# Edge steps of the mixing stage: three doubled instead of six, eight index places, a new order of the last loads, and the low half of the gathered sources on VectorE

## The reference

```python
xn = _layernorm(x, axis=-1)
x = x + gnn(xn) + mix(xn)      # below
x = x + ffn(_layernorm(x))     # eight experts, the best one per node, weighted by its gate

def _sage_conv(x, src, dst, W_l, W_r, b):
    n = x.shape[0]
    summed = jax.ops.segment_sum(x[src], dst, num_segments=n)
    deg = jax.ops.segment_sum(jnp.ones((src.shape[0],), x.dtype), dst, num_segments=n)
    agg = summed / jnp.maximum(deg, 1.0)[:, None]
    return agg @ W_l.T + x @ W_r.T + b

h = jnp.tanh(_sage_conv(xn, src, dst, W1_l, W1_r, b1))
gnn = _sage_conv(h, src, dst, W2_l, W2_r, b2)

z = 1.0 / jnp.einsum('bnhf,bhf->bnh', q_phi, k_phi.sum(axis=1))
mix = jnp.einsum('bnhf,bhfd,bnh->bnhd', q_phi, kv, z) @ w_proj + b_proj
```

## Time and profile before

| | before |
|---|---|
| median of 3 runs | 2524.41 us |
| profiled execution, its time | 2524.75 us |
| its span, first to last instruction | 2522.9 us |
| TensorE busy | 2373.8 us (94%) |
| VectorE busy | 1693.2 us (67%) |
| GpSimd busy | 1185.5 us (47%) |
| mixing stage, its products | about 1515 to 2121 us |

### The profile page before, as it was taken

The page is one execution under the profiler, slowest core; times in us unless marked ns, Lnnn a source line. Parts: engine busy times, 40 slices in busy tenths (PEclk is TensorE's granted clock), DMA queues, the critical chain, the costliest instruction groups (busy, mean ns, idle before and its releaser), DMA issues.

```text
span 2522.9 us, 37535 instructions
## 1 busy us (share of the span) xinstructions
PE 2373.8 (94%) x11499; PEld 1899.0 (75%) x11499; DVE 1693.2 (67%) x3522; ACT 1110.6 (44%) x2047; POOL 1185.5 (47%) x1087
## 2 busy tenths in 40 slices
PE   5899999999999999899999988989999997886997
PEld 4788888888888888688888865666777776664986
DVE  5577777777777774444443337778888784994676
ACT  3345554444444443343443433333332331664875
POOL 5576776666666664000000004555565551775444
PEclk8999999999999999999999998999999998998999
DMA  9865765555555554455445436887888777995885
GB/s 370 265 186 156 201 162 143 147 145 126 143 145 129 142 146 103 194 210 201 178 157 199 184 131 195 210 221 215 237 230 235 218 216 267 353 367 212 253 262 190
DMA packets 159280, 507.40 MB, mean 201 GB/s; under 512 B 30274, under 2 KB 30786, under 8 KB 127026
## 3 DMA queue, kind: packets, MB, share of 16 engines
q1 hardware_dynamic: 109380, 376.45, 41.7%
q0 software_dynamic: 49200, 128.35, 23.2%
q10 hardware_dynamic: 576, 1.07, 0.1%
HBM read 263.83 MB, written 241.96 MB: 200 GB/s over the span
## 4 chain that ended last, share of the span: by engine, by line
PE 82%; DMA 7%; DVE 3%; issue 3%; SPq 2%; ACT 2%; POOL 1%; ACTq 0%; POOLq 0%; DVEq 0%
PE bank L1352 54%; PE bank L1403 8%; PE bank L1359 6%; DMA agg_d<-O,eidx 4%; PE bank L1536 3%; PE bank L1612 3%; PE bank L1467 2%; PE bank L439 1%; PE bank L440 1%; ACT r_xn L962 1%; SPq L509 1%; PE bank L1602 1%; DVE pd L1182 1%; PE bank L1604 1%; DMA a_x<-in_x 1%
## 5 line engine op out<-in xcount | busy, mean ns | idle before, releaser
L400 POOL DMA_INDIRECT agg_d<-O,eidx x160 | 274.2, 1714 | 210.2 <-DMA agg_d<-O,eidx 144.6
L336 POOL TENSOR_TENSOR G_low<-G,G_high 128x512 fp32r<-128x512 f32 x160 | 235.2, 1470 | 237.8 <-ACT G_high L461 237.6
L383 POOL DMA_INDIRECT G<-y_d,esrc x80 | 87.4, 1093 | 527.6 <-DMA y_d<-b_y 514.9
L419 DVE SCALAR_TENSOR_TENSOR Sj<-erow,dstf,tri 128x128 f32<-128x128 int32 x160 | 195.2, 1220 | 46.2 <-DMA agg_d<-O,eidx 46.2
L461 ACT CAST G_high<-G 128x512 fp32r<-128x512 f32 x160 | 99.2, 620 | 190.3 <-DVE G L1067 176.9
L428 DVE SCALAR_TENSOR_TENSOR eidx<-cnt,todump,dstf 128x1 int32<-128x1 f32 x160 | 155.8, 974 | 7.6
L932 ACT CAST qz_high<-low 128x512 fp32r<-128x512 f32 x80 | 49.6, 620 | 232.8 <-PE bank L1352 149.5
L758 POOL TENSOR_TENSOR pd<-pd,low 128x512 f32<-128x512 f32 (+1 forms) x80 | 142.4, 1780 | 0.0
L336 POOL TENSOR_TENSOR a_xn_rows_low<-a_x,a_xn_rows_high 128x512 fp32r<-128x512 f32 x80 | 142.0, 1775 | 0.3 <-ACT a_xn_rows_high L830 0.3
L804 POOL DMA_INDIRECT out<-x_out,x_id x87 | 83.4, 959 | 113.8 <-DVE x_out L1314 111.4
L1352 PE MATMUL bank<-Wk_high,xnT_high 128*128 128x512 f32 x320 | 128.6, 402 | 6.3 <-DVE xnT_low L336 6.3
(11 more groups left out here) (224 smaller groups left out, 7297.5 us busy)
## 6 DMA issues: line engine op xcount, KB each, us to landing
x_rows<-xs_d SPq DMA_DIRECT2D x87, 260.0 KB, 3.1
agg_d<-zero SPq DMA_DIRECT2D x20, 1040.0 KB, 20.0
b_agg<-agg_d SPq DMA_DIRECT2D x20, 1040.0 KB, 8.8
a_x<-in_x SPq DMA_DIRECT2D x20, 1024.0 KB, 6.7
agg_d<-z_halves SPq DMA_DIRECT2D x20, 1024.0 KB, 5.9
q_d<-q_rows SPq DMA_DIRECT2D x80, 256.0 KB, 2.4
r_d<-r_rows SPq DMA_DIRECT2D x80, 256.0 KB, 3.7
r_in<-r_d SPq DMA_DIRECT2D x20, 1024.0 KB, 6.8
```

What stands on the lines that cost most here:

```text
L336: return eng.tensor_tensor(out_, full, high.bitcast(F32), ALU.subtract)
L383: pool.indirect_dma_start(G[:, j, :], None, table, bass.IndirectOffsetOnAxis(ap=esrc[:, b, j:j + 1], axis=0)).then_inc(e_g[j], 16)
L400: pool.indirect_dma_start(agg, bass.IndirectOffsetOnAxis(ap=eidx[:, j, 0:1], axis=0), O[:, j, 0:width], None, compute_op=ALU.add).then_inc ...
L419: dve.scalar_tensor_tensor(Sj[:, :], row, dstf[:, b, j:j + 1], tri[:, :], ALU.is_equal, ALU.mult, accum_out=cnt[:, j:j + 1]).then_inc(e_cn ...
```

## The change

In the plan of edge steps the doubled steps are now t = 12, 20 and 28; 29 edge steps are done by t = 31, and from 32 on edge step te runs in step te + 3. The index tile eidx gets eight places instead of four (place 4 * b + j), and `edge_build` waits in this stage for the scatter eight back. The low half G_low is made by VectorE, after hT_low and ahead of the reciprocal, and no longer by GpSimd. SyncE's last commands of the stage come in another order: the step that stores the last but one part tile goes ahead of `part_in(1, 1)`, the step that stores the last one and `part_in(3, 3)` go ahead of the wait for all scatters, and all four `agg_in` come after it; `part_in(2, 2)` stands ahead of `agg_in(2, 2)`.

```diff
@@ -225,7 +225,7 @@
         Sj = sb("Sj", [P, P])
         cnt = sb("cnt", [P, 4])
         cnt1 = sb("cnt1", [P, 4])
-        eidx = sb("eidx", [P, 4, 1], I32)
+        eidx = sb("eidx", [P, 8, 1], I32)
         O = sb("O", [P, 4, AW])
         est = sb("est", [P, 6])
 
@@ -345,7 +345,7 @@
 
         mix_edges, done = [], 0
         for t in range(32):
-            now = 0 if t < 6 else 1 + (t in (10, 14, 18, 22, 26, 30))
+            now = 0 if t < 6 else 1 + (t in (12, 20, 28))
             mix_edges.append([(s // 8, s % 8) for s in range(done, done + now)])
             done += now
         ahead = done - 32
@@ -392,12 +392,12 @@
         def edge_scatter(pool, ph, turn, k, agg, width):
             it = item(ph, turn, k, "scatter")
             if it:
-                i, _, _, j = it
+                i, _, b, j = it
                 if ph == 0 and isinstance(i, int) and i == 0:
                     pool.wait_ge(s_z1, 16 * NG)
                 need_apart(pool, e_o, ph * NT + i + 1)
                 need_apart(pool, e_sc, 16 * (ph * NT + i))
-                pool.indirect_dma_start(agg, bass.IndirectOffsetOnAxis(ap=eidx[:, j, 0:1], axis=0),
+                pool.indirect_dma_start(agg, bass.IndirectOffsetOnAxis(ap=eidx[:, 4 * b + j, 0:1], axis=0),
                                         O[:, j, 0:width], None, compute_op=ALU.add).then_inc(e_sc, 16)
 
         def edge_build(dve, ph, turn, k):
@@ -414,7 +414,7 @@
                 dve.tensor_scalar(todump[:, b, :], dstf[:, b, :], -1.0, trash[:, 0:1], ALU.mult, ALU.add
                                   ).then_inc(e_f, 1)
             need(dve, e_mm, u - 4)
-            need(dve, e_sc, 16 * (u - 4))
+            need(dve, e_sc, 16 * (u - (8 if ph else 4)))
             row = erow[:, b, j:GROUP:TG]
             dve.scalar_tensor_tensor(Sj[:, :], row, dstf[:, b, j:j + 1], tri[:, :], ALU.is_equal,
                                      ALU.mult, accum_out=cnt[:, j:j + 1]).then_inc(e_cnt, 1)
@@ -425,7 +425,7 @@
             dve.wait_ge(e_cnt, 2 * u)
             if j == 0:
                 dve.wait_ge(e_f, 2 * ug + 2)
-            dve.scalar_tensor_tensor(eidx[:, j, :], cnt1[:, j:j + 1], todump[:, b, j:j + 1],
+            dve.scalar_tensor_tensor(eidx[:, 4 * b + j, :], cnt1[:, j:j + 1], todump[:, b, j:j + 1],
                                      dstf[:, b, j:j + 1], ALU.mult, ALU.add).then_inc(e_s, 1)
 
         def edge_pe(pe, ph, turn, k, psum):
@@ -663,20 +663,19 @@
             sp.wait_ge(m_st[0], 16 * (PAIRS - 1))
             sp.wait_ge(m_qz, NT)
             part_in(0, 0)
+            mix(PAIRS, 5)
             sp.wait_ge(e_mm, 2 * NT)
             part_in(1, 1)
+            mix(PAIRS + 1, 1)
+            sp.wait_ge(m_p, NT)
+            part_in(3, 3)
             sp.wait_ge(e_sc, 16 * 2 * NT)
             agg_in(0, 0)
-            mix(PAIRS, 5)
-            sp.wait_ge(m_p, NT - TG)
             agg_in(1, 1)
-            mix(PAIRS + 1, 1)
-            sp.wait_ge(m_p, NT)
+            sp.wait_ge(m_st[1], 16 * PAIRS)
+            part_in(2, 2)
             agg_in(2, 2)
             agg_in(3, 3)
-            part_in(3, 3)
-            sp.wait_ge(m_st[1], 16 * PAIRS)
-            part_in(2, 2)
             sp.wait_ge(m_st[0], 16 * PAIRS)
 
 
@@ -772,7 +771,6 @@
                 t = 8 * turn + k
                 edges = edge_steps(turn, k)
                 for te in edges:
-                    edge_low(pool, 1, *te)
                     edge_gather(pool, 1, *te, y_d.ap())
                 for te in edges:
                     edge_scatter(pool, 1, *te, agg2_d.ap(), D)
@@ -1175,6 +1173,8 @@
                     dve.wait_ge(m_hh, t - 3)
                     low_half(dve, mhT[1][:, kk // 4, kk % 4, :], hT[:, kk // 4, kk % 4, :],
                              mhT[0][:, kk // 4, kk % 4, :]).then_inc(m_hl, 1)
+                for te in edge_steps(turn, k):
+                    edge_low(dve, 1, *te)
                 if active(t, 0, NT) and k % 4 == 0:
                     g = 2 * turn + k // 4
                     dve.wait_ge(m_den, g + 1)
```

## The result

The changed kernel took 2531.85 us (median of 20 executions, 2524.78 to 2538.52), the kernel before, run beside it on the same chips, 2524.00 (20 executions, 2517.56 to 2538.27). The ratio is 1.0022, 95% interval 1.0012 to 1.0032: slower by 3 to 8 us, where 11 us less was forecast. One execution differs from the next by several us whatever the kernel: here everything ahead of the stretch in question ends 3.9 us earlier after (1526.96 against 1530.81), and the profiled execution of the changed kernel is 3.5 us under its median. So I go by the lengths of stretches, not by spans.

What follows compares the result with a forecast made beforehand. TensorE, busy 94% of the span, was taken as the bound, with 35.2 us idle early: -35.2 + 2.1 + 4.7 + 8.3 + 8.9 = -11.2, from 2524.75 to 2513.5 us; range 2499 to 2533.

Steps and rivals of the forecast that it cites:

- rival (b): Early steps: scatters stay the bound and only three are saved, 2528.2 us, or some 2521 with their room; chance 0.20.
- TensorE as the bound early: Steps with doubled edge steps and a little after: all 35.2 us of TensorE's idle time go; bounds 20.6 and 35.2.
- 6.6 us a scatter: Early groups: 5.8 + 0.8 us per scatter, so 4.5 edges take 29.7 us a group against TensorE's 28.5 + 0.2.
- the steady stall: Eleven steady groups: G_low in VectorE's order makes TensorE's edge sum late, mean 0.75 us a group, 8.3 us in all.
- The run of 11.3 us: VectorE's work from hT_high's start to the second G_low; the sum is late by hT_high's delay after the product minus 5.0.
- VectorE gets less busy: With G_low moved, qz_low and Sj lose 57 us of stretching against 48 us of new work on VectorE.
- rival (e): GpSimd: each scatter's issue is longer by 0.5 us, +6 on the forecast, 2519.5 us; chance 0.07.
- the end: After the last m_x: store, part 3 and aggregate 0 queue in a row, so routing's first addition comes 8.9 us later.
- (a): Edge sums: the new G_low on VectorE is never late, 2500.5 us; chance 0.17.
- (c): Scatters: all slow to 7.5 us from issue to issue, making the kernel slower, 2544 us; chance 0.09.
- (d): End of the stage: the aggregates' delay is hidden, 2504.6 us; chance 0.05.

Runs made afterwards that it cites:

- experiment 5: Single parts of the change alone on the kernel before; eight index places alone: 2517.47 us, ratio 0.9965, and again 2519.98 us, 0.9980.
- experiment 2: The changed kernel with G_low back on GpSimd ahead of the gather, all else as changed: 2524.69 us, ratio 0.9996 to the kernel before.
- experiment 1: The changed kernel with SyncE's old order of the last loads, all else as changed: 2529.81 us, ratio 1.0008 to the kernel before.
- the quarter load: The changed kernel loading only a quarter of hT, used for all four steps, part of the input left out: one execution, steps 36 to 76 in 288.3 us.

## Why the prediction was wrong, step by step

The sum was -11.2; the result is about +5.6 by the ratio, an interval of 0.2% where I had reckoned with 0.5%. The measured median, 2531.85, lies inside the stated range only by its high end, which was made from rival (b), not from what happened. By stretches, with TensorE's 4.08 matmuls per us and the prediction's own stalls, it comes to this: steps 8 to 12, 90 matmuls and 2.1 us: 24.2; 12 to 36, 703 matmuls and 4.7 us: 177.0; 36 to 76, 284.7 + 10 x 0.75 = 292.2; the last, 75.9 + 1.5 for six matmuls + 0.8 = 78.2. The forecasts of the table add up to -9.5, not -11.2: cut this way the idle time before is 33.3 us instead of 35.2, as far as a count of matmuls is good at the edges of a window.

| stretch | before | forecast | after | missed by |
|---|---|---|---|---|
| 8 to 12 | 24.3 | 24.2 | 26.6 | +2.4 |
| 12 to 36 | 205.1 | 177.0 | 181.2 | +4.2 |
| 36 to 76 | 284.7 | 292.2 | 300.4 | +8.2 |
| 76 to last m_x | 75.9 | 78.2 | 80.0 | +1.8 |
| last m_x to first row | 1.7 | 10.6 | 10.7 | +0.1 |

**Right: TensorE as the bound early.** That the idle time would go as a whole, and not 20.6 us of it, came true. In steps 12 to 36 after, TensorE waits 5.7 us for G_low on VectorE (4.7 forecast) and 1.5 us in its own queue in the three doubled steps, and never for a sum O, an index or a landing. With the 2.5 us of step 9 that is all of the 9.8 us that it is idle from step 8 to 36. Rival (b), scatters as the bound, falls; that its 2528.2 us is the time of the profiled execution is chance. But two steps that led there were wrong. I took 6.6 us a scatter, and they are 7.2 us apart; it did no harm, since the looser waits carry the queue over the doubled groups. And I read from one place in a timeline that TensorE hangs on G_low behind a scatter; over steps 12 to 36 before, it waited 1.6 us for G_low and 13.2 for eidx on VectorE, which the eight places alone free (experiment 5). Where G_low stays on GpSimd (experiment 2) the same pace costs 13.0 us.

**Right: the mechanism of the steady stall; wrong: its size.** "A mean stall of 0.75 us a group" is the term that failed. Measured are 1.57 us a group, (300.4 - 284.7) / 10, and three things make up the difference of 0.82.
- The edge, some 0.4 us a group. I took the sum to be late from 5.0 us of hT_high's delay on. In the groups that run evenly after the change hT_high starts 5.0 to 5.1 us after the product and they take 28.8 to 29.0 us in place of 28.5: the edge is nearer 4.6. The run of 11.3 us from hT_high to the sum is 11.5 in the chain shown above; that is half of it.
- The load, some 0.25 us a group. The mean delay of 5.75 was right for before (5.8 over the ten groups), but after it is 6.1, and it reaches further out: 9.2 and 8.7 us, where before had at most 7.5. These two groups take 34.6 and 32.5 us and have 10.1 of the 15.7 us. In the first of them the first G_low is late too (TensorE waits 1.1 us at 1746.1, ahead of the 3.1 at 1755.5).
- The clock, 0.17 us a group. The stall at 1752 is followed by the lower clock, which costs another 1.7 us. That term stood nowhere in the sum. It is most of the miss in steps 8 to 12, whose mean granted clock is 0.94 where it was 1.00: 0.06 x 26.6 = 1.6 us. The rest there is idle time, 2.5 us (26.6 less 24.1 busy) where 2.1 were forecast. The last stretch, too, has 0.98: 1.6 us.

The 2.4 us a group that I gave as the upper bound held for the mean, not for single groups (6.2 and 4.0 us). The cost is a difference of two numbers of nearly the same size, hT_high's start and the edge, each known to some half a us, and nothing in the trace of before could tell how late the loads would land once groups and edge steps had shifted against each other.

**Right: VectorE gets less busy.** The groups by line, busy us and mean ns, which answer to the earlier trace rows:

```profile
L400 POOL DMA_INDIRECT agg_d<-O,eidx x80 | 130.0, 1625 | 282.7 <-DMA agg_d<-O,eidx 174.2 <-ACT O L449 71.0 <-issue 23.6
...
L336 DVE TENSOR_TENSOR qz_low<-low,qz_high 128x512 fp32r<-128x512 f32 x80 | 54.7, 684 | 0.1
L336 DVE TENSOR_TENSOR G_low<-G,G_high 128x512 fp32r<-128x512 f32 x80 | 54.5, 684 | 0.0
...
L419 DVE SCALAR_TENSOR_TENSOR Sj<-erow,dstf,tri 128x128 f32<-128x128 int32 x80 | 35.3, 441 | 0.0
```

qz_low falls from 1028 to 684 ns and Sj from 799 to 441, 56 us in the two, as worked out (57). But VectorE is 59 us less busy in all, not 9 (57 less the 48 of new work): other forms had been stretched as well, dstf (1022 to 199 ns, 16 us), eidx (461 to 220, 19 us) and hT_low (797 to 689, 9 us). A longer issue of the scatters, rival (e), doesn't show: 1625 ns in the mean where it was 1667, beside 80 more instructions with two SBUF inputs. The Trainium skill, SBUF — State Buffer, bears on both. The first agrees with its exclusive lock. For the second I had read it too widely: its section "Who interferes with whom" says that a VectorE instruction with two SBUF inputs contends with a GpSimd instruction that reads SBUF, which G_low does; of a `tensor_tensor` it says that it takes the read interface alone, and of the making of descriptors, as inferred, that it needs the write interface. The trace agrees: no longer issue.

**Right: the end.** 8.9 us forecast, 9.0 measured, with the aggregate landing 9.1 us after its issue. What I hadn't seen is that this isn't the order's alone: in the old order, with the sums three steps later, 5 of the 9 us are lost as well (experiment 1).

**The rivals.** (a), no stall: wrong, and it is what the quarter load comes near to in the steady stretch. (c), slower by scatters at 7.5 us: the scatters came within 0.3 us of that and TensorE didn't wait for them; the kernel is slower by another way, of which no rival told: the forecast's own mechanism at twice its price. (d): wrong, the wait is there in full. (b) and (e) are answered above.

## What to carry to other kernels

An instruction put into an engine's queue behind one that waits for a load inherits that load's lateness; if it feeds the engine that sets the time, cost it by the spread of the landings and not by their mean, allow for a spread that the change itself widens, and add to each longer stall the slower clock that often follows. Undo parts one at a time: of the parts here one (eight index places) was a gain that the sum of the others hid, and the kernel with the lowest ratios is the kernel before with that part alone, 0.9965 and 0.9980 of its time. Where a lag puts work at the end of a stage, reordering the loads behind it may give back little: here 4 of 9 us.

## What the runs showed of the hardware

- **The load lands later where more shares its flight.** In the kernel after, hT's load of 1 MB, from issue to hT_high's start, mostly took 4.8 us (once 5.2) where gathers and scatters moved 0.02 to 0.2 MB in that time, 6.2 to 6.3 us with 0.4 to 0.6 MB, 7.8 us with 0.5 MB and 0.8 MB of other loads or stores, and 8.5 to 9.0 us with 0.7 MB and 0.3 MB of those, so that the amount alone doesn't set it. With a quarter of it hT_high starts 3.7 to 4.3 us after the product's end, with the whole 4.9 at best. Which of the transfers holds up which isn't shown.
- **A gap of TensorE often costs more than its length.** From step 8 on the fourteen profiles have 40 gaps of 2.4 us or more in this stage, and after 35 of them the next 3.5 us have a mean granted clock of 0.50 to 0.67; in the kernel after those ahead of 1539.67 (2.5 us), 1755.54 (3.1) and 2066.6 (2.5), not the one ahead of 1819.08 (3.0). Part of the early loss of the kernel before is this: steps 12 to 36 have a mean granted clock of 0.97 there, 0.03 x 205.1 = 6.2 us, and 1.00 after.
- **Scatters start about 7 us apart.** Over the whole stage the mean is 6.9 to 7.2 us in every kernel. From step 32 on that is the program's own pace, four in a group of 28.5 us. In the first 27 it is 6.6 to 7.0 where six steps are doubled and 7.1 to 7.5 where three to five are, with G_low in GpSimd's queue or without. What sets it there is not settled; hT's load is at most a part.
